# Two typed slabs in place of one byte slab: shared buffers and later loads in a sandwich transformer layer on 8 cores

## The chip, the cores and the metric

The kernel runs on the 8 cores of one Trainium2 chip, with one launch for the whole layer. Each core works for itself: there is no transfer between cores. The metric is the device time of the slowest core in microseconds.

## The reference

The layer takes `x` of 4 x 2048 tokens x 2048 features. Attention has 32 query heads and 8 key/value heads of 64, with rotary embedding and a causal mask; the FFN has 8-bit weights held as integers, 8192 wide.

```python
x = x + layernorm(attention(layernorm(x), wq, wk, wv, wo))
x = x + layernorm(ffn(layernorm(x), gate_w, gate_scale, up_w, up_scale, down_w, down_scale))
# attention: q, k, v = x@wq, x@wk, x@wv; rope(q), rope(k); softmax(q k^T / 8, causal) v; @wo
# ffn: W = (w_int - 128) * scale per output row; h = silu(x Wg^T) * (x Wu^T); h Wd^T
```

## The kernel before

A core owns 1024 of the 2048 tokens of one batch entry: 64 of every 128. It computes K and V for all 2048 tokens of that entry and everything else for its own. There is no scheduler: each engine's program is the sequence of its blocks in the order in which the Python code emits them, and all that holds engines apart are waits on five counters. `pt`, `pv`, `ps` count PE, DVE and ACT; `dx` counts the transfers issued by SP, `dw` those issued by POOL. `Prog.inc` adds to a counter and `wait_ge(c.dx.sem, c.dx.n)` waits for every transfer issued on that queue so far. A name such as `v_krope[t]` is the value of `pv` at which a step is done. So a wait emitted on a queue also holds everything that is emitted on that queue behind it.

On chip memory is one byte tensor, `slab`, of 197,120 bytes per partition, in which each buffer is a bitcast view at a fixed offset, and beside it a number of small tensors: the rotary tables `qcos_s`, `qsin_s`, `kcos_s`, `ksin_s`, the scales `gsc_s`, `usc_s`, the selection matrix `selm` and others.

The stages, in order:

- **Prelude** (`emit_prelude`): SP loads ten small constants and tables and waits for all (L267, L268); POOL loads `eye_b`.
- **Phase A** (`emit_phase_a`): POOL loads `wk_p`, then `wv_p`. 16 tiles t of 128 tokens: SP loads `xt` (L326, two buffers; tile t waits for `v_ln1[t-2]`), DVE takes statistics (L222, L226), ACT computes `rstd` (L230, L233), DVE normalizes (L346). Two tiles later, `emit_a1(t)`: PE transposes (L359), ACT copies out (L368, L372), PE projects K and V (L383, L386), DVE applies the rotation from `kcos_s` and `ksin_s` and keeps the key norms (L246 to L407, whose last is `v_krope[t]`), PE transposes K (L420), ACT copies it out. The loop emits `emit_a0(t)` and then `emit_a1(t - 2)`, so `emit_a1(7)` stands behind `emit_a0(9)` and ahead of `emit_a0(10)` on every queue.
- **Phase A2** (`emit_phase_a2`): for each half h, POOL loads 1024 columns of `wq_p` once phase A is done; PE projects Q (L484), DVE rotates it and sums its squares, PE transposes it, ACT copies it out.
- **Phase B** (`emit_phase_b`): a bound of the scores per row, then 32 heads `qh`, 16 blocks `cc` of 128 keys each: PE scores (L756), ACT exp (L768), DVE mask (L777), PE product with V (L719 to L726). At a head's end DVE copies the denominators (L792, L793) and the product (L795, L796) into `rawatt`, ACT inverts the denominators (L802, L805), and inside the next head (`emit_tail`, ahead of block 4) PE spreads the reciprocals over partitions (L683, L685), DVE copies them to `rbs` (L692) and multiplies into `att_fm` (L698). `rbs` and both `rawatt` lie on partitions 64 to 127.
- **Phase C** (`emit_phase_c`): the output projection (L871, POOL loads `wo_p` in two halves), then 8 blocks p of 128 tokens: SP loads `xown` to `xo` (L926), DVE adds the layernorm (L947, L951) into `x2t`, SP stores it to `x2scr` (L960), and it is normalized again, transposed and copied to `ln3_fm`.
- **Phase D** (`emit_phase_d`): column sums of `ln3_fm` on PE (L1034), spread and scaled (L1043, L1050, L1057), which carry the zero point of 128; then 64 blocks `ib`: POOL loads `wg_p` and `wu_p` (L1080, L1082, one after the other), PE computes gate and up (L1098, L1103), DVE subtracts (L1117, L1119), ACT applies silu (L1125), DVE multiplies (L1132). Then sums over `hdn` (L1142), the down scales spread over partitions (L1173, copied by L1180), and the down projection in 64 loads of `wd_p` (L1194, L1208), each quarter closed by a product with `m128f` (L1214).
- **Phase E** (`emit_phase_e`): 8 blocks p: SP loads the kept rows from `x2scr` to `x2r` (L1255), DVE takes statistics of `y`, normalizes into `ot` (L1274) and adds `x2r` (L1278), SP stores `ot` (L1285). Every load and store on SP waits for all dx transfers before it.

## Time and profile before

| | us |
|---|---|
| median of 2 runs | 3516.13 (3512.64 to 3519.62) |
| the profiled execution | 3343.91 |
| its span, slowest core (core 2) | 3342.4 |
| its spans, all cores | 3312.1 to 3342.4 |

| engine, core 2 | busy us | share of the span |
|---|---|---|
| PE | 2406.5 | 72% |
| PE weight loads (beside PE) | 1075.6 | 32% |
| DVE | 960.6 | 29% |
| ACT | 664.1 | 20% |
| POOL | 108.0 | 3% |

PE is busy for most of the span, but the stages differ, so a share of the whole span says little about one place. The views used are: the busy time by stretch, which shows the limit of each stage; the timeline, in which each instruction stands with its start, its duration and, in brackets, how long its engine was idle before and what released it; and the groups by form, which give the mean duration of one instruction. Times count from the start of the span.

### The profile page before, as it was taken

What the parts mean: (1) busy time and instruction counts of PE and PEld (TensorE: products, weight loads), DVE (VectorE), ACT (ScalarE), POOL (GpSimd) and SP (SyncE); (2) the same over time, 40 slices, a digit from 0 to 9 for tenths busy, and PEclk for the clock granted to TensorE, in tenths of its full rate; (3) what the DMA queues carried; (4) which work ended last, traced back from release to release, by engine and by line L of the source; (5) the groups of instructions that cost most, each with busy time, mean ns of one, the idle gap of its engine ahead of it and who ended that gap; (6) DMA issues with size and microseconds to landing.
All of it is one profiled execution on the core that took longest, in us unless ns stands there. A gap on an engine that the chain in (4) does not pass through costs nothing.

```text
span 3342.4 us, 28537 instructions; the slowest of 8 cores (3312.1 to 3342.4 us)
## 1 busy us (share of the span) xinstructions
PE 2406.5 (72%) x10358; PEld 1075.6 (32%) x10358; DVE 960.6 (29%) x1647; ACT 664.1 (20%) x1307; POOL 108.0 (3%) x203
## 2 busy tenths in 40 slices
PE   2555355356777777655717999999999989999960
PEld 1222122122322332222413444444444434444420
DVE  4444133233444444400173222222222200000024
ACT  1222112114666666500121000000000000000000
POOL 0000000000000000000000000000000000000000
PEclk9777687676676676678958999999999999999885
DMA  5110300300000000033044444444444424334324
GB/s 138 50 51 26 49 2 3 48 0 1 1 1 1 1 1 1 13 51 51 0 151 89 76 77 77 76 78 76 76 76 76 70 40 74 63 63 76 58 69 163
DMA packets 44984, 174.90 MB, mean 52 GB/s; under 512 B 5033, under 2 KB 5425, under 8 KB 38449
## 3 DMA queue, kind: packets, MB, share of 16 engines
q0 software_dynamic: 36336, 121.68, 22.0%
q1 hardware_dynamic: 8514, 51.40, 4.3%
q8 instruction: 88, 1.44, 0.2%
q14 instruction: 46, 0.38, 0.0%
HBM read 277.89 MB, written 16.78 MB: 88 GB/s over the span
## 4 chain that ended last, share of the span: by engine, by line
PE 66%; DVE 13%; DMA 9%; ACT 7%; issue 5%; DVEq 0%; ACTq 0%; SPq 0%; POOLq 0%
PE psA L1098 13%; PE psB L1103 13%; PE psA L1208 7%; PE psB L1208 7%; PE psA L484 5%; PE psA L871 3%; ACT slab L768 3%; PE psA L756 3%; PE psB L383 2%; PE psB L722 2%; PE psB L386 2%; DMA slab<-wq_p 2%; DMA slab<-wo_p 2%; PE psB L719 2%; DVE stat L222 2%
## 5 line engine op out<-in xcount | busy, mean ns | idle before, releaser
L1098 PE MATMUL psA<-slab 128*128 128x512 bf16 x2048 | 464.5, 380 | 2.9 <-DVE slab L1057 1.5
L1103 PE MATMUL psB<-slab 128*128 128x512 bf16 x2048 | 462.9, 379 | 0.0
L1208 PE MATMUL psA<-slab 128*128 128x512 bf16 x1024 | 268.2, 385 | 17.9 <-DVE slab L1225 15.4
L1098 PEld LDWEIGHTS psA<-slab 128*128 128x128 bf16 x2048 | 200.3, 98 | 247.4 <-issue 8.5
L1103 PEld LDWEIGHTS psB<-slab 128*128 128x128 bf16 x2048 | 200.4, 98 | 241.7
L1208 PE MATMUL psB<-slab 128*128 128x512 bf16 x1024 | 266.8, 383 | 0.0
L768 ACT ACTIVATE slab<-psA 128x1024 bf16<-128x1024 f32 (+7 forms) x352 | 226.2, 660 | 135.6 <-PE psA L756 132.7
L1117 DVE TENSOR_TENSOR slab<-psA,slab 128x1024 f32<-128x1024 f32 x64 | 78.4, 1224 | 574.0 <-PE psB L1103 574.0
L1125 ACT ACTIVATE slab<-slab,gsc_s 128x1024 bf16<-128x1024 f32 x64 | 73.5, 1148 | 830.7 <-DVE slab L1119 830.7
L484 PE MATMUL psA<-slab 128*128 128x512 bf16 x512 | 171.0, 508 | 64.4 <-DMA slab<-wq_p 64.4
L719 PE MATMUL psB<-slab 128*65 128x512 bf16 (+3 forms) x256 | 114.6, 448 | 123.7 <-DVE slab L777 123.2
L756 PE MATMUL psA<-slab 65*128 65x512 bf16 (+3 forms) x544 | 184.6, 416 | 4.9 <-DMA slab<-rowv 4.8
L383 PE MATMUL psB<-slab 128*128 128x512 bf16 x256 | 115.6, 452 | 84.8 <-ACT slab L372 84.8
L871 PE MATMUL psA<-slab 128*128 128x512 bf16 x512 | 119.7, 388 | 68.2 <-DMA slab<-wo_p 68.2
L230 ACT ACTIVATE lntmp<-mv,epsv 128x1 f32<-128x1 f32 x40 | 12.0, 300 | 749.1 <-DVE mv L226 749.1
L1225 DVE TENSOR_TENSOR slab<-psA,slab 128x512 bf16<-128x512 f32 x16 | 9.9, 682 | 491.3 <-PE psB L1214 491.3
L1208 PEld LDWEIGHTS psA<-slab 128*128 128x128 bf16 x1024 | 101.0, 99 | 147.0 <-issue 29.6
L722 PE MATMUL psB<-slab 128*65 128x512 bf16 x256 | 145.2, 567 | 0.0
L1208 PEld LDWEIGHTS psB<-slab 128*128 128x128 bf16 x1024 | 101.3, 99 | 124.4 <-issue 6.3
L513 PE MATMUL psB<-eye_b,slab 128*128 128x128 bf16 x128 | 13.9, 238 | 148.0 <-DVE qn L500 148.0
L386 PE MATMUL psB<-slab 128*128 128x512 bf16 x256 | 114.7, 448 | 0.0
L484 PEld LDWEIGHTS psA<-slab 128*128 128x128 bf16 x512 | 62.2, 125 | 159.2 <-issue 138.4
(126 smaller groups left out, 2172.2 us busy)
## 6 DMA issues: line engine op xcount, KB each, us to landing
slab<-wg_p POOLq DMA_DIRECT2D x64, 512.0 KB, 5.2
slab<-wu_p POOLq DMA_DIRECT2D x64, 512.0 KB, 5.9
slab<-wd_p POOLq DMA_DIRECT2D x64, 512.0 KB, 5.2
slab<-xb SPq DMA_DIRECT2D x16, 1024.0 KB
slab<-wq_p POOLq DMA_DIRECT2D x2, 4096.0 KB, 33.8
slab<-xown SPq DMA_DIRECT2D x8, 1024.0 KB
slab<-wo_p POOLq DMA_DIRECT2D x2, 4096.0 KB, 33.0
x2scr<-slab SPq DMA_DIRECT2D x8, 1024.0 KB
```

What stands on the lines that cost most here:

```text
L383: e.matmul(c.bank(4), fm[t % 2][:, dm * 128:(dm + 1) * 128], c.wk_b[:, dm * 512:(dm + 1) * 512], start=(dm == 0), stop=(dm == 15))
L386: ins = e.matmul(c.bank(5), fm[t % 2][:, dm * 128:(dm + 1) * 128], c.wv_b[:, dm * 512:(dm + 1) * 512], start=(dm == 0), stop=(dm == 15))
L484: ins = e.matmul(c.bank(ob), c.pairfm[:, dm * 1024 + p * 128:dm * 1024 + (p + 1) * 128], wqh[:, dm * 1024 + ob * 512:dm * 1024 + (ob + 1) ...
L719: e.matmul(pvb[0][:, p0 * 128:512], lhs, pbf[:, OFFC[cc]:OFFC[cc] + wA], start=(cc == 0), stop=(cc == 7), skip_group_check=True)
L722: ins = e.matmul(pvb[1][:, 0:512], lhs, pbf[:, OFFC[cc] + wA:OFFC[cc] + N], start=(cc == 0), stop=(cc == 15), skip_group_check=True)
L756: ins = e.matmul(s2[si][:, half * 512:half * 512 + n], c.k65[:, kv * 2048 + cc * 128:kv * 2048 + (cc + 1) * 128], c.q65[:, qh * 1024 + p0 ...
L768: ins = e.activation(out=pbuf[qh % 2][:, OFFC[cc]:OFFC[cc] + N], in_=s2[si][:, 0:N], func=ACT.Exp, bias=0.0, scale=1.0)
L871: ins = e.matmul(c.bank(idx % 2), woh_buf[:, dm * 1024 + do * 128:dm * 1024 + (do + 1) * 128], c.att_fm[:, dm * 1024 + grp * 512:dm * 1024 ...
L1098: e.matmul(gbank[:, half * 512:(half + 1) * 512], wgt[ib % 2][:, hc * 128:(hc + 1) * 128], c.ln3_fm[:, hc * 1024 + half * 512:hc * 1024 + ...
L1103: ins = e.matmul(ubank[:, half * 512:(half + 1) * 512], wut[ib % 2][:, hc * 128:(hc + 1) * 128], c.ln3_fm[:, hc * 1024 + half * 512:hc * 1 ...
L1117: ins = e.tensor_tensor(out=gtmp[:], in0=gbank, in1=c.cs3[:, :], op=OP.subtract)
L1208: ins = e.matmul(c.bank(tt), c.hdn[:, ic * 1024 + tt * 128:ic * 1024 + (tt + 1) * 128], wdt[gi % 3][:, ici * 512:(ici + 1) * 512], start=( ...
```

## The change

The byte slab becomes two slabs of fixed types: `slb`, 92,288 bf16 columns, and `slf`, 5,632 float32 columns. Buffers that were bitcast views become slices. The float32 slab is small, so more buffers share space, some are dropped, and several small tensors move into it:

- The K tables hold half their columns. SP loads the first half in the prelude, and the second in phase A, emitted behind `emit_a1(7)`; tile 8's rotation waits for it.
- The Q tables and `selm` are no longer loaded in the prelude but by POOL at the start of phase A2, ahead of `wq_p`, with a wait for them. `gsc_s` and `usc_s` are loaded by POOL ahead of `wg_p[0]`, with a wait.
- `rawatt` is gone: DVE copies the product with V straight to `att_fm` and multiplies it there in place. `rbs` becomes two buffers, on partitions 0 to 63 for even heads and 64 to 127 for odd ones. One wait of DVE moves from ahead of L792 to ahead of L692, and one is added ahead of L698.
- `xo` and `x2t` have one buffer each in place of two, with waits to match.
- `m128f` is set right before the copy of the down scales. The copy to `s3` waits for the dx transfers.
- `ot` is gone: in phase E DVE works in halves of 1024 columns, normalizing into `ln4b` and adding into `x2r`, which is stored.

```diff
--- before.py
+++ after.py
-        c.qcos_s = sb("qcos_s", [128, 256], F32)
-        c.qsin_s = sb("qsin_s", [128, 256], F32)
-        c.kcos_s = sb("kcos_s", [128, 512], F32)
-        c.ksin_s = sb("ksin_s", [128, 512], F32)
-        c.gsc_s = sb("gsc_s", [128, 64], F32)
-        c.usc_s = sb("usc_s", [128, 64], F32)
...
-        SLAB = 197120
-        c.slab = top.enter_context(nc.sbuf_tensor("slab", [128, SLAB], mybir.dt.uint8))
-
-        def view(off, cols, dt, parts=128):
-            esz = mybir.dt.size(dt)
-            return c.slab[0:parts, off:off + cols * esz].bitcast(dt)
-
...
-        c.rbs = c.slab[64:128, 188928:193024].bitcast(F32)
-        c.rawatt = [c.slab[64:128, 184832:186880].bitcast(BF16),
-                    c.slab[64:128, 186880:188928].bitcast(BF16)]
...
-        c.xo = [view(147968, 2048, F32), view(156160, 2048, F32)]
-        c.x2t = [view(164352, 2048, F32), view(172544, 2048, F32)]
...
-        c.x2r = [view(32768, 2048, F32), view(40960, 2048, F32)]
-        c.ot = [view(49152, 2048, F32), view(57344, 2048, F32)]
...
+        c.slb = top.enter_context(nc.sbuf_tensor("slb", [128, NBELS], BF16))
+        c.slf = top.enter_context(nc.sbuf_tensor("slf", [128, NFELS], F32))
+
+        def viewb(off, cols, parts=128):
+            return c.slb[0:parts, off:off + cols]
+
+        def viewf(off, cols, parts=128):
+            return c.slf[0:parts, off:off + cols]
+
...
+        c.xt = [viewf(0, 2048), viewf(2048, 2048)]
+        c.rt1 = viewf(4096, 512)
+        c.rt2 = viewf(4608, 512)
+        c.kcos_s = viewf(5120, 256)
+        c.ksin_s = viewf(5376, 256)
+        c.qcos_s = viewf(0, 256)
+        c.qsin_s = viewf(256, 256)
+        c.qt1 = viewf(4096, 512)
...
+        c.qn2 = viewf(2048, 256)
+        c.selm = viewf(2304, 256, parts=8)
+        c.sqt = viewf(4096, 128)
+        c.sq2 = viewf(4224, 128)
+        c.dens = viewf(0, 1024, parts=1)
+        c.lntmp2 = viewf(1024, 1024, parts=1)
+        c.rbs2 = [c.slf[0:64, 2560:3584], c.slf[64:128, 2560:3584]]
...
+        c.xo = [viewf(0, 2048)] * 2
+        c.x2t = [viewf(2048, 2048)] * 2
+        c.gsc_s = viewf(5120, 64)
+        c.usc_s = viewf(5184, 64)
...
+        c.us = c.ubf
+        c.y = viewb(0, 16384)
+        c.gtmp = viewf(0, 1024)
+        c.cs3 = viewf(2048, 1024)
+        c.s3 = viewf(3072, 1024, parts=1)
+        c.sdn = viewf(3072, 1024, parts=1)
+        c.m128f = viewf(2048, 512, parts=1)
+        c.dsc_s = viewf(0, 2048, parts=1)
+        c.dsc_bc = viewf(0, 2048)
+        c.x2r = [viewf(0, 2048), viewf(2048, 2048)]
+        c.ln4b = viewf(4096, 1024)
...
     @block.sync
     def _(e):
         for dst, srcap in [(c.eye_f, c.eye), (c.mA, c.maskA), (c.mB, c.maskB),
-                           (c.qcos_s, c.qcos), (c.qsin_s, c.qsin),
-                           (c.kcos_s, c.kcos), (c.ksin_s, c.ksin),
-                           (c.gsc_s, c.gsc), (c.usc_s, c.usc),
-                           (c.selm, c.selmap)]:
+                           (c.kcos_s, c.kcos[:, 0:256]),
+                           (c.ksin_s, c.ksin[:, 0:256])]:
             c.dx.inc(e.dma_start(out=dst[:], in_=srcap), 16)
         e.wait_ge(c.dx.sem, c.dx.n)
...
-        e.memset(c.onescb[:], 1.0)
-        c.pv.inc(e.memset(c.m128f[:], -128.0))
+        c.pv.inc(e.memset(c.onescb[:], 1.0))
...
-            c.pv.inc(_rope(c, e, c.bank(4), 8, c.kcos_s[:, t * 32:(t + 1) * 32],
-                           c.ksin_s[:, t * 32:(t + 1) * 32], krot[:], rt1, rt2))
+            if t == 8:
+                e.wait_ge(c.dx.sem, c.dx_kh)
+            tm = t % 8
+            c.pv.inc(_rope(c, e, c.bank(4), 8, c.kcos_s[:, tm * 32:(tm + 1) * 32],
+                           c.ksin_s[:, tm * 32:(tm + 1) * 32], krot[:], rt1, rt2))
...
+        if t == 7:
+            @block.sync
+            def _(e):
+                e.wait_ge(c.pv.sem, v_krope[7])
+                e.wait_ge(c.dx.sem, c.dx.n)
+                c.dx.inc(e.dma_start(out=c.kcos_s[:], in_=c.kcos[:, 256:512]), 16)
+                c.dx.inc(e.dma_start(out=c.ksin_s[:], in_=c.ksin[:, 256:512]), 16)
+                c.dx_kh = c.dx.n
...
             if h == 1:
                 e.wait_ge(c.pt.sem, t_q[(0, 7, 1)])
             e.wait_ge(c.dw.sem, c.dw.n)
+            if h == 0:
+                c.dw.inc(e.dma_start(out=c.qcos_s[:], in_=c.qcos), 16)
+                c.dw.inc(e.dma_start(out=c.qsin_s[:], in_=c.qsin), 16)
+                c.dw.inc(e.dma_start(out=c.selm[:], in_=c.selmap), 16)
+                e.wait_ge(c.dw.sem, c.dw.n)
             ins = e.dma_start(out=wqh[:].rearrange("p (a b) -> p a b", a=16),
                               in_=c.wq_p[:, :, h * 1024:(h + 1) * 1024])
             dwq[h] = c.dw.inc(ins, 16)
...
             e.wait_ge(c.pt.sem, t_bc[qh])
-            ins = e.tensor_copy(out=c.rbs[:, :], in_=s2[0][0:64, 0:1024])
+            if (qh - 2) in v_att:
+                e.wait_ge(c.pv.sem, v_att[qh - 2])
+            rbsv = c.rbs2[qh % 2]
+            ins = e.tensor_copy(out=rbsv, in_=s2[0][0:64, 0:1024])
             v_rbs[qh] = c.pv.inc(ins)
             e.wait_ge(c.pv.sem, v_rbs[qh])
+            e.wait_ge(c.pv.sem, v_raw[qh])
             j = qh // 2
             r0 = (qh % 2) * 64
             dst = c.att_fm[r0:r0 + 64, j * 1024:(j + 1) * 1024]
-            ins = e.tensor_tensor(out=dst[:, :], in0=c.rawatt[qh % 2][:, :],
-                                  in1=c.rbs[:, :], op=OP.mult)
+            ins = e.tensor_tensor(out=dst[:, :], in0=dst[:, :],
+                                  in1=rbsv, op=OP.mult)
             v_att[qh] = c.pv.inc(ins)
...
-            if (qh - 2) in v_att:
-                e.wait_ge(c.pv.sem, v_att[qh - 2])
             e.tensor_copy(out=c.dens[0:1, 0:512], in_=pvb[0][64:65, 0:512])
             ins = e.tensor_copy(out=c.dens[0:1, 512:1024], in_=pvb[1][64:65, 0:512])
             v_dens[qh] = c.pv.inc(ins)
-            e.tensor_copy(out=c.rawatt[qh % 2][:, 0:512], in_=pvb[0][0:64, 0:512])
-            ins = e.tensor_copy(out=c.rawatt[qh % 2][:, 512:1024], in_=pvb[1][0:64, 0:512])
+            j = qh // 2
+            r0 = (qh % 2) * 64
+            dst = c.att_fm[r0:r0 + 64, j * 1024:(j + 1) * 1024]
+            e.tensor_copy(out=dst[:, 0:512], in_=pvb[0][0:64, 0:512])
+            ins = e.tensor_copy(out=dst[:, 512:1024], in_=pvb[1][0:64, 0:512])
...
-            if p < 2:
+            if p == 0:
                 e.wait_ge(c.pv.sem, c.v_att_all)
                 e.wait_ge(c.pt.sem, bar_pt)
                 e.wait_ge(c.ps.sem, bar_ps)
             else:
-                e.wait_ge(c.pv.sem, v_x2[p - 2])
+                e.wait_ge(c.pv.sem, v_x2[p - 1])
...
+            if p >= 1:
+                e.wait_ge(c.pv.sem, v_l3[p - 1])
...
+        e.wait_ge(c.dx.sem, c.dx.n)
         c.pv.inc(e.tensor_copy(out=s3[:], in_=c.psA[0:1, 0:1024]))
...
+            if ib == 0:
+                c.dw.inc(e.dma_start(out=c.gsc_s[:], in_=c.gsc), 16)
+                c.dw.inc(e.dma_start(out=c.usc_s[:], in_=c.usc), 16)
+                e.wait_ge(c.dw.sem, c.dw.n)
             c.dw.inc(e.dma_start(out=wgt[ib % 2][:], in_=c.wg_p[ib]), 16)
             e.wait_ge(c.dw.sem, c.dw.n)
             ins = e.dma_start(out=wut[ib % 2][:], in_=c.wu_p[ib])
...
         e.wait_ge(c.pt.sem, c.pt.n)
+        e.wait_ge(c.pv.sem, v_h[63])
+        e.memset(c.m128f[:], -128.0)
         c.pv.inc(e.tensor_copy(out=c.dsc_bc[:], in_=c.psA[:, :]))
...
-            c.pv.inc(e.tensor_scalar(out=ot[p % 2][:], in0=yv[:, p, :],
-                                     scalar1=c.mv[:, 0:1], scalar2=c.rstd[:, 0:1],
-                                     op0=OP.subtract, op1=OP.mult))
-            e.wait_ge(c.pv.sem, c.pv.n)
-            ins = e.tensor_add(ot[p % 2][:], ot[p % 2][:], x2r[p % 2][:])
-            v_o[p] = c.pv.inc(ins)
+            for half in range(2):
+                c.pv.inc(e.tensor_scalar(
+                    out=c.ln4b[:], in0=yv[:, p, half * 1024:(half + 1) * 1024],
+                    scalar1=c.mv[:, 0:1], scalar2=c.rstd[:, 0:1],
+                    op0=OP.subtract, op1=OP.mult))
+                e.wait_ge(c.pv.sem, c.pv.n)
+                sl = x2r[p % 2][:, half * 1024:(half + 1) * 1024]
+                v_o[p] = c.pv.inc(e.tensor_add(sl, sl, c.ln4b[:]))
+                if half == 0:
+                    e.wait_ge(c.pv.sem, v_o[p])
...
-            c.dx.inc(e.dma_start(out=c.out[p * 128:(p + 1) * 128, :], in_=ot[p % 2][:]), 16)
+            c.dx.inc(e.dma_start(out=c.out[p * 128:(p + 1) * 128, :], in_=x2r[p % 2][:]), 16)
```

## Rows read from the trace of the kernel before

**Rows 1.** Spans by core: span in us, mean granted TensorE clock.

```profile
core 2: 3342.4 us, clock 0.830
```

**Rows 2.** Windows: stretch, length, PE, PEld, DVE, ACT, POOL busy, PEclk, DMA share, GB/s.

```profile
780.00:1415.00 635.00, 459.64 (x1610) 191.93 (x1610) 276.44 (x709) 382.79 (x587) 0.00 (x0) 0.68 0.00 1
...
1779.00:2716.00 937.00, 926.98 (x4260) 415.31 (x4259) 235.52 (x195) 75.83 (x66) 67.67 (x128) 0.99 0.43 72
...
3235.00:3342.40 107.40, 0.00 (x0) 0.00 (x0) 50.36 (x56) 3.98 (x16) 0.00 (x0) 0.50 0.43 156
```

**Rows 3.** Timeline, start: start us, us, engine, line, instruction [idle before].

```profile
1.56 0.66 POOL L272 DMA_DIRECT2D eye_b<-eye  x1 [0.86 <-POOLq L44]
...
5.50 0.53 POOL L301 DMA_DIRECT2D slab<-wk_p  x1 [3.28 <-DMA eye_b<-eye]
...
43.69 1.87 PE L359 MATMUL psA<-eye_b,slab 128*128 128x128 bf16 x16 [43.69 <-DMA slab<-wv_p]
```

**Rows 4.** Chain that ended last, start of phase A: start us, us, what.

```profile
43.87 5.63 DMA slab<-xb
```

**Rows 5.** Timeline, phase A around tile 10; xN rows start at their first.

```profile
181.92 63.30 SPq L326 DMA_DIRECT2D slab<-xb  x4
...
218.42 0.17 DVE L407 TENSOR_TENSOR knm<-knm,kn 128x8 f32<-128x8 f32 x1
...
219.10 2.46 DVE L222 BATCH_NORM_STATS2 stat<-slab 128x6 f32<-128x512 f32 x4
...
222.41 0.20 ACT L233 ACTIVATE rstd<-lntmp 128x1 f32<-128x1 f32 x1
...
222.63 2.05 ACT L368 CAST slab<-psA 128x512 bf16<-128x512 f32 x4
```

**Rows 6.** Timeline, start of phase A2.

```profile
421.00 4.90 PE L484 MATMUL psA<-slab 128*128 128x512 bf16 x16 [34.89 <-DMA slab<-wq_p]
...
426.01 0.42 DVE L246 TENSOR_TENSOR slab<-psA,qcos_s 128x256 f32<-128x256 f32 x1 [39.94 <-PE psA L484]
```

**Rows 7.** Timeline, start of phase D.

```profile
1780.01 0.55 POOL L1080 DMA_DIRECT2D slab<-wg_p  x1 [237.30 <-issue]
...
1787.67 1.21 DVE L1043 COPY slab<-psA 1x1024 f32<-1x1024 f32 x1 [13.15 <-PE psA L1034]
...
1791.09 1.22 DVE L1057 TENSOR_SCALAR slab<-psB 128x1024 f32<-128x1024 f32 x1 [2.21 <-PE psB L1050]
...
1791.20 0.53 POOL L1080 DMA_DIRECT2D slab<-wg_p  x1 [5.09 <-DMA slab<-wu_p]
...
1792.46 5.24 PE L1098 MATMUL psA<-slab 128*128 128x512 bf16 x16 [1.48 <-DVE slab L1057]
```

**Rows 8.** Timeline, start of the down projection.

```profile
2724.34 1.86 PE L1208 MATMUL psA<-slab 128*128 128x512 bf16 x4 [2.54 <-DVE slab L1180]
```

**Rows 9.** Groups by form: line, engine, shapes | busy us, mean ns | idle.

```profile
L1117 DVE TENSOR_TENSOR slab<-psA,slab 128x1024 f32<-128x1024 f32 x64 | 78.4, 1224 | 574.0 <-PE psB L1103 574.0
...
L280 DVE MEMSET m128f<- 1x512 f32 x1 | 0.5, 485 | 0.1
```

**Rows 10.** Timeline, one block of phase E.

```profile
3254.59 1.34 DVE L1274 TENSOR_SCALAR slab<-slab,mv,rstd 128x2048 f32<-128x2048 bf16 x1 [6.91 <-DMA slab<-x2scr]
...
3256.03 2.29 DVE L1278 TENSOR_TENSOR slab<-slab 128x2048 f32<-128x2048 f32 x1
...
3258.46 0.34 SPq L1285 DMA_DIRECT2D out<-slab  x1
```

**Rows 11.** Timeline, DVE in the attention: one instruction per head, four of them.

```profile
990.26 1.22 DVE L692 COPY slab<-psA 64x1024 f32<-64x1024 f32 x1 [0.95 <-PE psA L685]
...
1008.89 1.22 DVE L692 COPY slab<-psA 64x1024 f32<-64x1024 f32 x1 [0.95 <-PE psA L685]
...
1260.33 1.22 DVE L692 COPY slab<-psA 64x1024 f32<-64x1024 f32 x1 [0.95 <-PE psA L685]
...
1280.51 1.22 DVE L692 COPY slab<-psA 64x1024 f32<-64x1024 f32 x1 [0.95 <-PE psA L685]
```

76 lines of the change are left out of this document (29 added, 47 removed).

## The prediction

> **What bounds the kernel now.** I read the spans by core first, then the busy time by stretch, then the timeline at each place that the diff touches. Core 2 is the slowest, with a span of 3342.4 us and a mean granted clock of 0.830 [rows 1]; the profiled execution took 3343.9 us. The median of the runs shown is 3516.13 us, 172 us (5.2%) more. No row says where these 172 us lie, so the sum is made against 3343.9 and then laid on the median.
>
> The stages run one after the other. The attention (785 to 1415 us) is a loop of latencies between PE, ACT and DVE in which no engine is full: PE 460, ACT 383, DVE 276 of 635 us, at a granted clock of 0.68 of the full 2.4 GHz, so a mix of both levels [rows 2]. The FFN's up part is PE's: 927 of 937 us busy, at 0.99 [rows 2]. In the last 107.4 us PE does nothing, DVE works 50.4 us, and the transfer engines are busy for 0.43 of it [rows 2]: store and load take turns with DVE. So the question for each edit is whether it sits in PE's full stretches (where only PE counts) or in one of the serial places, where each microsecond shows.
>
> **Prelude.** SP issues 5 small loads instead of 10, so the first x tile comes a little sooner. But PE's first matmul waits for wv_p, at 43.69 us, behind eye_b and wk_p on POOL's queue [rows 3], which the edit leaves alone. Value 0. The bounds are 0 and a gain of 2.5 us: some 0.6 MB less to move beside wk_p, where an x tile of 1 MB takes 5.63 us alone [rows 4], and not all of it falls beside wk_p.
>
> **Phase A, the second half of the K tables.** The cost lies in where SP's block was put. Between load x[9] and load x[10] SP gets a wait on v_krope[7] and two loads. Load x[10] hung on v_ln1[8] until now and went out at 181.92 us; v_krope[7] ends at 218.42 + 0.17 = 218.59 [rows 5]. Then come two issues, about 0.5 us each, and load x[10] at about 219.65. A tile alone takes 5.63 us [rows 4]: landing at 225.3, and up to 1.4 us later if the 256 KB of tables share the engines with it (a quarter of 5.63). DVE started its stats of tile 10 at 219.10 [rows 5]. That is 6.2 to 7.6 us late; I take 6.7. Who is behind it: rstd of tile 10 on ACT, and on ACT the copies L368 of tile 8, which start right behind rstd's second step (222.41 + 0.20) at 222.63 [rows 5]; PE's projections of tile 8 wait for those copies. rstd is what they wait for already, so no cover is left, and the stall passes in full, once: **+6.7**. Load x[11] then goes out near 226, long before its own stats one tile later; nothing else is late.
>
> **Phase A2, tables and selm on POOL.** Three small loads and a wait for them now stand ahead of the first wq_p load, for which PE waits 34.89 us [rows 6]: nothing covers them. The nearest row is eye_b on the same queue: 0.66 us of issue, 3.28 us of idle until it has landed, and wk_p's issue starts 3.94 us after eye_b's [rows 3]. Two more issues at 0.6 us make 5.1 us at the least; the upper bound takes the wait behind a 512 KB weight load, 5.09 us [rows 7], and one more microsecond for the tables' 256 KB: 8.0. These loads carry more than eye_b and far less than a weight tile, so I stay near the lower end: **+5.5**. The Trainium skill, DMA: Bandwidth & Descriptors, section "Anatomy of one DMA — SWDGE (gpsimd) path", gives about 2.0 us plus bytes by 436 GB/s for one such load; by it this term would be an estimated 4.2 us and the whole sum 1 to 3 us less. eye_b's row contradicts it by 1.3 us, and the row is used.
>
> **Phase D, gate and up scales on POOL.** Two loads and a wait stand ahead of wg_p[0], which went out at 1780.01 [rows 7]. By eye_b's row it goes 3.94 + 0.55 = 4.5 us later. The cover: wu_p[0] had landed by 1791.20, while DVE's L1057, for which PE waits too, ended at 1791.09 + 1.22 = 1792.31 [rows 7]. 1.1 us are hidden: **+3.4** (bounds 2.8, if the second issue costs nothing, and 5.2, with 5.09 for the wait). Block 1's pair (two loads of 5.09 + 0.53) then lands near 1807, before PE asks for it one block (927 / 64 = 14.5 us) after 1795.9: no second stall. A rule speaks against moving loads to POOL: by the Trainium skill, SBUF — State Buffer, the warning about the "DVE blocks DMA" trap, the descriptors of gpsimd loads aren't written while DVE runs in a two-port mode. DVE sat idle for 39.94 us before 426.01 and for 13.15 us before 1787.67 [rows 6, 7], so by this trace it would add nothing.
>
> **m128f.** The memset moves from the start to a place right before the copy L1180, for which PE waits [rows 8]; it took 485 ns [rows 9]: **+0.5**.
>
> **Phase E, halves.** Each of the 8 blocks was L1274 1.34, a gap of 0.10, L1278 2.29, and the store's issue 0.13 later: 3.87 us from 3254.59 to 3258.46 [rows 10]. A tensor_tensor over 1024 takes 1.22 (L1117 [rows 9]), one over 2048 takes 2.29, so 1.05 ns an element and 0.15 fixed. L1274 at 1.34 for 2048 goes at half that per element: 1.07, and 0.27 fixed; 1024 take 0.81 (bounds 0.67, half of it, and 1.22, as slow as L1117). Two halves: 2 x (0.81 + 0.10 + 1.22) + 0.10 + 0.13 = 4.49, so 0.62 more per block. SP's order is load, store, load, and each waits for the one before, with DVE between: all 8 count, **+4.9** (bounds 2.7 and 11.5).
>
> **Attention.** One wait on DVE is taken from before L792 and two are put beside L692 and L698, each on work long done; DVE's gaps with a met wait are the 0.10 us of [rows 10], so at most 0.1 x 32 = 3 us either way. Value 0. But the heads aren't alike: from L692 to L692 one takes 18.63 us and another 20.18 [rows 11], the ends of the 30 gaps between whole heads, with the same work. If the shift of everything before them moved all heads to one end, it would be half the spread, 0.8 x 32 = 25 us, either way.
>
> **Edits at nothing.** Typed slabs for byte views: each instruction keeps element types and shapes, so the rows' durations stand, and buffers that now share space are held apart by written waits, so only these count. Phase C's single `xo` and `x2t`: SP's order is load p, store p, load p+1, and load p+1 waits for store p, so it never ran ahead; the new waits are met when reached. The wait on all dx before the s3 copy: the last store of x2scr is cover enough behind the transposes and L1034; without that cover it is at most a tile's 5.6 us. Phase E in place: store p has ended before load p+1 goes out, so the missing `ot` blocks nothing.
>
> **Sum:** 6.7 + 5.5 + 3.4 + 0.5 + 4.9 = 21.0 us. On the profiled execution 3343.9 + 21 = 3365; on the median 3516.1 + 21 = **3537 us**, 0.6% more. The terms are latencies of transfers and DVE, so I lay them on the median unscaled.
>
> **The rivals.** (1) *The stalls are hidden.* If tile 10 were needed later than I read and POOL's loads landed in a microsecond, phase E's 4.9 and some of the rest stay: about +9, 3525 us. Against it: consumers already wait at these places [rows 5, 6]. Chance 0.12. (2) *The attention's rhythm moves.* For it: heads of equal work differ by 1.5 us; against it: 32 heads even it out. At its ends 3512 and 3562 us; chance 0.12, evenly split. (3) *Slower beyond 2%: the in-place product.* L795 and L796 now write `att_fm`, L698 reads and writes the same addresses, and even heads have their reciprocals on partitions 0 to 63. If L692 and L698 took double, 2.44 us more per head with the masks L777 queued behind them and PE waiting for the masks, 32 heads cost 78 us: 3615 us. It decides from 1.5 us per head on, (70 - 21) / 32. Against it: shapes and types are unchanged. Chance 0.05. (4) *The median moves to the profiled level.* The profiled execution ran 172 us below the median; if the changed kernel's runs stood there, 3365 us would be shown, 4.3% faster, nothing of it due to the diff. Chance 0.04.
>
> **How the numbers follow.** The sum's own case has the remaining 0.67. Within 2% of 3516 (3446 to 3586; two percent is about what a measurement of this kernel can tell from no change) lie the sum, rival 1 and rival 2: 0.91. Faster has 0.04, slower 0.05. The sum's own bounds: A 6.2 to 7.6, A2 5.1 to 8.0, D 2.8 to 5.2, E 2.7 to 11.5, prelude -2.5 to 0, so 3531 to 3549. The range takes in the attention's rhythm on both sides with a little for the waits: 3508 to 3572; it leaves out rivals 3 and 4.
>
> **What would show it.** In the profile after: the stats of tile 10 begin near 225.8, their wait put down to the x load, and phase A ends 6 to 7 us later; PE's wait for wq_p grows from 35 to about 40 us; PE's first L1098 waits some 3.4 us for a weight transfer instead of for L1057; a memset of 0.49 us before L1180's copy; phase E's halves at 0.81 and 1.22, its blocks 0.6 us further apart. The attention from its first L692 to its last stays within 10 us, with L692 and L698 at 1.22. I am wrong if L777, L692 or L698 get longer, if PE's full stretches change by more than their first wait, or if the timed runs stand at another level than before.

## The result and the profile after

| | before | after |
|---|---|---|
| median of all runs | 3381.6 us (20 runs, from 3339.9) | 3362.2 us (21 runs, from 3348.1) |
| ratio of after to before, with its 95% interval | | 1.0035 [1.0022, 1.0049] |
| profiled execution | 3343.9 us | 3367.5 us |
| its spans, all cores | 3312.1 to 3342.4 us | 3315.7 to 3365.9 us |

The changed kernel is slower by 0.35%, which is some 12 us of 3345, and counts as the same by 2%. The direction and the class are as predicted; the number, 3537 us, and its range are not: 3362 us lies far below 3508. In a good part of the runs of either kernel one die shows a lower granted clock and the time is longer, which by their times holds for both runs behind the 3516 us; the others take 3340 to 3350 us for the kernel before, and the ratio is made of such runs alone.

The spans of the two slowest cores and the medians of the two dies of the changed kernel; they answer to [rows 1]:

```profile
core 5: 3361.6 us, clock 0.826
core 6: 3365.9 us, clock 0.826
...
die 0 (median of its cores): 3332.4 us, clock 0.833
die 1 (median of its cores): 3354.5 us, clock 0.827
```

Its slowest cores are not typical ones. On core 6 the down projection took 541.6 us and on core 7 538.4, from the load of the down scales to the first load of phase E, against 521.8 on the median core. The windows of core 5 and then of core 6, the same stretch of that stage (cores 0 and 4 are at 0.95 there like core 5, core 7 at 0.88 like core 6):

```profile
core 5: us, PE busy (x) PEld busy (x) DVE busy (x) ACT busy (x) POOL busy (x), PEclk, DMA share, GB/s
...
3050.00:3200.00 150.00, 144.87 (x636) 64.43 (x635) 4.87 (x8) 0.00 (x0) 10.04 (x19) 0.95 0.42 69
```

```profile
core 6: us, PE busy (x) PEld busy (x) DVE busy (x) ACT busy (x) POOL busy (x), PEclk, DMA share, GB/s
...
3050.00:3200.00 150.00, 144.06 (x574) 61.84 (x585) 4.87 (x8) 0.00 (x0) 8.98 (x17) 0.88 0.38 63
```

PE is as busy in both and gets fewer matmuls done at the lower clock (574 and 636). The repetition of the changed kernel (`e9`) does not have this. It is a part of why the profiled executions stand 23.5 us apart where the timed runs stand 12. From here on stages are compared as means over the eight cores, each stage from its first instruction to that of the next (worked out from the timelines of all cores):

| stage, mean over the cores, us | before | after |
|---|---|---|
| start to PE's first matmul | 44.6 | 45.2 |
| to the first load of `wq_p` (phase A; after, the POOL loads too) | 341.6 | 353.4 |
| phase A2 and the bounds of phase B | 393.2 | 391.0 |
| attention and the first half of phase C | 880.9 | 875.4 |
| first store of `x2scr` to first load of `wg_p` | 107.1 | 110.5 |
| gate and up | 935.2 | 933.5 |
| down projection | 521.0 | 526.1 |
| phase E | 101.0 | 104.0 |

The windows that answer to [rows 2], core 6:

```profile
core 6: us, PE busy (x) PEld busy (x) DVE busy (x) ACT busy (x) POOL busy (x), PEclk, DMA share, GB/s
780.00:1415.00 635.00, 461.63 (x1621) 192.45 (x1619) 274.58 (x713) 382.86 (x590) 0.00 (x0) 0.70 0.00 1
1779.00:2716.00 937.00, 919.37 (x4171) 415.17 (x4253) 235.36 (x194) 78.06 (x70) 68.77 (x130) 0.99 0.42 72
3259.00:3365.90 106.90, 0.00 (x0) 0.00 (x0) 54.15 (x73) 3.98 (x16) 0.00 (x0) 0.50 0.40 157
```

Attention and FFN look much as before (the same stretch of time begins some 9 us earlier in the program here). DVE's 54.15 us in the last window stand against 50.36 [rows 2]: the halves.

**Tile 10** (timeline, answers to [rows 5]):

```profile
216.91 0.17 DVE L408 TENSOR_TENSOR knm<-knm,kn 128x8 f32<-128x8 f32 x1
...
217.21 0.33 SPq L444 DMA_DIRECT2D slf<-kcos  x1
...
217.59 0.43 SPq L445 DMA_DIRECT2D slf<-ksin  x1
...
218.16 12.85 SPq L324 DMA_DIRECT2D slf<-xb  x3
...
225.59 2.47 DVE L223 BATCH_NORM_STATS2 stat<-slf 128x6 f32<-128x512 f32 x4 [7.91 <-DMA slf<-xb]
...
228.91 0.20 ACT L234 ACTIVATE rstd<-lntmp 128x1 f32<-128x1 f32 x1
229.13 2.05 ACT L366 CAST slb<-psA 128x512 bf16<-128x512 f32 x4
```

The load of tile 10 goes out behind the two table loads, DVE sits idle for 7.91 us before the statistics (5.6 to 8.5 on the eight cores, 6.9 on average; nothing was there before), and ACT's copies of tile 8 stand right behind that rstd.

**The POOL loads** (timeline, POOL and PE at the start of phase A2, then POOL, DVE and PE at the start of phase D; they answer to [rows 6, 7]):

```profile
395.38 0.54 POOL L479 DMA_DIRECT2D slf<-qcos  x1 [370.75 <-PE psB L421]
...
396.45 0.52 POOL L481 DMA_DIRECT2D slf<-selmap  x1
398.85 1.17 POOL L483 DMA_DIRECT2D slb<-wq_p  x1 [1.87 <-DMA slf<-selmap]
431.47 5.72 PE L499 MATMUL psA<-slb 128*128 128x512 bf16 x15 [36.78 <-DMA slb<-wq_p]
```

```profile
1782.41 0.57 POOL L1104 DMA_DIRECT2D slf<-gsc  x1 [234.77 <-issue]
...
1782.97 0.55 POOL L1105 DMA_DIRECT2D slf<-usc  x1
...
1785.72 0.54 POOL L1107 DMA_DIRECT2D slb<-wg_p  x1 [2.19 <-DMA slf<-usc]
...
1793.31 1.22 DVE L1080 TENSOR_SCALAR slf<-psB 128x1024 f32<-128x1024 f32 x1 [2.21 <-PE psB L1073]
...
1797.36 3.19 PE L1125 MATMUL psA<-slb 128*128 128x512 bf16 x7 [4.16 <-DMA slb<-wu_p]
```

`wq_p` goes out 3.5 us behind the first POOL issue on this core (3.9 on the mean of the eight) and `wg_p` 3.3 us. PE's first gate matmul, which waited for the sums before (1.48 <-DVE in [rows 7]), now waits for a weight transfer.

**`m128f` and phase E** (timeline, answers to [rows 8, 10]):

```profile
2725.10 0.48 DVE L1208 MEMSET slf<- 1x512 f32 x1 [5.74 <-PE psA L1200]
2725.51 2.22 DVE L1209 COPY slf<-psA 128x2048 f32<-128x2048 f32 x1
```

```profile
3273.11 0.32 SPq L1284 DMA_DIRECT2D slf<-x2scr  x1
3277.91 0.81 DVE L1304 TENSOR_SCALAR slf<-slb,mv,rstd 128x1024 f32<-128x1024 bf16 x1 [6.05 <-DMA slf<-x2scr]
3278.83 1.23 DVE L1310 TENSOR_TENSOR slf<-slf 128x1024 f32<-128x1024 f32 x1
...
3282.22 2.46 DVE L223 BATCH_NORM_STATS2 stat<-slb 128x6 f32<-128x512 bf16 x4
3282.43 0.34 SPq L1318 DMA_DIRECT2D out<-slf  x1
```

From the start of the first half to the issue of the store are 4.52 us, against 3.87 before.

### The profile page after: what moved, and what is told of

It reads as the page before. It is cut to its first block, busy times and chain, and to the rows that moved or that the text cites. A ratio compares the mean times of both kernels' runs of the same rounds, so it can differ in the third digit from the quotient of the medians.

```text
span 3365.9 us, 28447 instructions; the slowest of 8 cores (3315.7 to 3365.9 us)
## 1 busy us (share of the span) xinstructions
PE 2413.8 (72%) x10190; PEld 1082.1 (32%) x10358; DVE 962.8 (29%) x1663; ACT 664.7 (20%) x1307; POOL 110.7 (3%) x208
## 4 chain that ended last, share of the span: by engine, by line
PE 66%; DVE 13%; DMA 8%; ACT 7%; issue 5%; DVEq 0%; ACTq 0%; SPq 0%; POOL 0%; POOLq 0%
PE psA L1125 13%; PE psB L1130 13%; PE psA L1237 7%; PE psB L1237 7%; PE psA L499 5%; PE psA L891 3%; ACT slb L787 3%; PE psA L775 3%; PE psB L384 2%; PE psB L741 2%; PE psB L381 2%; DMA slb<-wq_p 2%; DMA slb<-wo_p 2%; PE psB L738 2%; DVE stat L223 2%
## 5 line engine op out<-in xcount | busy, mean ns | idle before, releaser
L1125 PE MATMUL psA<-slb 128*128 128x512 bf16 x2007 | 461.6, 380 | 6.3 <-DMA slb<-wu_p 4.2
L1130 PE MATMUL psB<-slb 128*128 128x512 bf16 x2007 | 459.9, 379 | 2.2
L1237 PE MATMUL psA<-slb 128*128 128x512 bf16 x1002 | 274.6, 396 | 20.4 <-DVE slb L1254 15.8
L1125 PEld LDWEIGHTS psA<-slb 128*128 128x128 bf16 x2048 | 200.8, 98 | 247.6 <-issue 7.7
L1130 PEld LDWEIGHTS psB<-slb 128*128 128x128 bf16 x2048 | 200.4, 98 | 241.6
L1237 PE MATMUL psB<-slb 128*128 128x512 bf16 x1004 | 273.6, 394 | 1.2
L787 ACT ACTIVATE slb<-psA 128x1024 bf16<-128x1024 f32 (+7 forms) x352 | 226.7, 660 | 135.3 <-PE psA L775 132.7
L1144 DVE TENSOR_TENSOR slf<-psA,slf 128x1024 f32<-128x1024 f32 x64 | 78.4, 1225 | 574.6 <-PE psB L1130 574.6
L1152 ACT ACTIVATE slb<-slf 128x1024 bf16<-128x1024 f32 x64 | 73.4, 1148 | 831.1 <-DVE slb L1146 831.1
L499 PE MATMUL psA<-slb 128*128 128x512 bf16 x499 | 169.3, 509 | 66.4 <-DMA slb<-wq_p 64.7
L738 PE MATMUL psB<-slb 128*65 128x512 bf16 (+3 forms) x256 | 115.0, 449 | 123.5 <-DVE slb L796 123.5
L775 PE MATMUL psA<-slb 65*128 65x512 bf16 (+3 forms) x544 | 184.4, 416 | 4.8 <-DMA slb<-rowv 4.8
L384 PE MATMUL psB<-slb 128*128 128x512 bf16 x256 | 115.9, 453 | 87.7 <-ACT slb L370 87.7
L891 PE MATMUL psA<-slb 128*128 128x512 bf16 x496 | 119.2, 390 | 63.3 <-DMA slb<-wo_p 62.5
L1237 PEld LDWEIGHTS psA<-slb 128*128 128x128 bf16 x1024 | 103.2, 101 | 155.2 <-issue 61.1
L741 PE MATMUL psB<-slb 128*65 128x512 bf16 x256 | 146.0, 570 | 0.0
L1237 PEld LDWEIGHTS psB<-slb 128*128 128x128 bf16 x1024 | 103.4, 101 | 131.2 <-issue 36.1
L528 PE MATMUL psB<-eye_b,slb 128*128 128x128 bf16 x128 | 13.7, 236 | 148.0 <-DVE slf L515 148.0
L381 PE MATMUL psB<-slb 128*128 128x512 bf16 x241 | 108.0, 448 | 10.6 <-ACT slb L370 10.6
L499 PEld LDWEIGHTS psA<-slb 128*128 128x128 bf16 x512 | 62.2, 125 | 159.6 <-issue 138.9
```

The lines of the kernel that those rows point to most:

```text
L381: e.matmul(c.bank(4), fm[t % 2][:, dm * 128:(dm + 1) * 128], c.wk_b[:, dm * 512:(dm + 1) * 512], start=(dm == 0), stop=(dm == 15))
L384: ins = e.matmul(c.bank(5), fm[t % 2][:, dm * 128:(dm + 1) * 128], c.wv_b[:, dm * 512:(dm + 1) * 512], start=(dm == 0), stop=(dm == 15))
L499: ins = e.matmul(c.bank(ob), c.pairfm[:, dm * 1024 + p * 128:dm * 1024 + (p + 1) * 128], wqh[:, dm * 1024 + ob * 512:dm * 1024 + (ob + 1) ...
L738: e.matmul(pvb[0][:, p0 * 128:512], lhs, pbf[:, OFFC[cc]:OFFC[cc] + wA], start=(cc == 0), stop=(cc == 7), skip_group_check=True)
L741: ins = e.matmul(pvb[1][:, 0:512], lhs, pbf[:, OFFC[cc] + wA:OFFC[cc] + N], start=(cc == 0), stop=(cc == 15), skip_group_check=True)
L775: ins = e.matmul(s2[si][:, half * 512:half * 512 + n], c.k65[:, kv * 2048 + cc * 128:kv * 2048 + (cc + 1) * 128], c.q65[:, qh * 1024 + p0 ...
```

## The experiments

The theory is the prediction's sum: the change adds five small serial stalls, each worth its own microseconds, and nothing else. Its rivals: the stalls are covered (rival 1), the attention moves (rival 2), the in-place product costs (rival 3). All ratios are to the kernel before, with 95% intervals.

### The second half of the K tables, taken out of the way and put in alone

`e1` is the changed kernel with the table loads emitted one tile later, behind the load of tile 10; the load of tile 11 waits for them.

```diff
-        if t == 7:                       # in emit_a1
-            <SP: wait v_krope[7]; load kcos, ksin second half>
+        if t == 10:                      # in the loop, behind emit_a0(10)
+            emit_kh()
```

> The changed kernel with one block moved: SP's wait for v_krope[7] and its two loads of the second half of the K tables are emitted behind the load of x tile 10 instead of ahead of it, and the load of tile 11 waits for the tables. Theory (the queue position costs, not the tables): DVE no longer idles before its stats of tile 10 (5.6 to 8.5 us on the eight cores of the changed kernel, mean 6.9), phase A from PE's first matmul to the first wq_p issue shrinks by 6.9 us in the mean over cores, and the kernel's time goes from a ratio of 1.0035 to about 1.0015. Rival (the tables' transfer or the missing half costs): the stall only moves to tile 8's rotation or to tile 11, and phase A stays within 2 us of the changed kernel's.

Measured: 1.0019 [1.0006, 1.0033]. SP (timeline of `e1`, core 4) and then DVE:

```profile
215.70 0.33 SPq L444 DMA_DIRECT2D slf<-kcos  x1
216.08 0.42 SPq L445 DMA_DIRECT2D slf<-ksin  x1
218.86 5.48 SPq L324 DMA_DIRECT2D slf<-xb  x2
```

```profile
216.08 2.47 DVE L223 BATCH_NORM_STATS2 stat<-slf 128x6 f32<-128x512 f32 x4
```

The tables still go out at the same place, but tile 10 is there, and its statistics begin without idle time (no bracket). From tile 1's key norm to the last one the eight cores take 294.2 us on the mean, against 293.8 before, and 300.4 to 303.7 with the block where the change has it (`e2`, `e9` and the changed kernel). In the stretch that the expectation names, PE's first matmul to the first `wq_p`, it is 343.3 us, 10.1 less than in the changed kernel and 5.3 less than in its repetition `e9`.

`e11` is the reverse: the kernel before, with the tables loaded in halves at the change's place.

```diff
-                           (c.kcos_s, c.kcos), (c.ksin_s, c.ksin),
+                           (c.kcos_s[:, 0:256], c.kcos[:, 0:256]),
+                           (c.ksin_s[:, 0:256], c.ksin[:, 0:256]),
...
+        if t == 9:
+            <SP: wait v_krope[7]; load the second halves>
```

> The kernel before with the K tables loaded in halves exactly where the change does it (SP's wait for v_krope[7] and two loads behind the load of tile 9), into the full-size tables. Theory (the stall of tile 10 passes in full to phase A's end): DVE stalls 5.5 to 8.5 us before tile 10, phase A from PE's first matmul to the first wq_p issue grows from 341.6 us by 6 to 7, ratio 1.0020. Rival (part of it is made up in the following tiles, as PE runs at another mix of its two clock levels): phase A grows by 4 us or less.

Measured: 1.0018 [1.0007, 1.0029], and 302.0 us from tile 1's key norm to the last, 8.2 more than before. In the stretch that the expectation names it is 347.4 us, 5.9 more than before: the part of it that lies ahead of tile 1's norm is 2.5 us shorter in `e11`, whose prelude loads half of the K tables less. Its DVE on the slowest core, the place of tile 10:

```profile
224.88 2.47 DVE L222 BATCH_NORM_STATS2 stat<-slab 128x6 f32<-128x512 f32 x4 [7.60 <-DMA slab<-xb]
```

So this part alone makes the stall and is worth 6 to 8 us, whichever kernel it stands in. On a single core it comes in two sizes. Without the stall a core takes 293.2 to 293.9 us from norm to norm, and now and then 296.1; with it 299.7 to 300.5, or 302.8 to 303.6, so some 6.5 or 9.5 us more (two cores of the changed kernel took longer still, see below). How many cores do which differs from run to run, and why was not tested.

### The loads moved to POOL

`e2` is the changed kernel with the Q tables, `selm` and the two scales loaded by SP at the end of phase A, on buffers that are free by then.

```diff
-                c.dw.inc(e.dma_start(out=c.qcos_s[:], in_=c.qcos), 16)   # and qsin, selm
-                e.wait_ge(c.dw.sem, c.dw.n)
...
+        e.wait_ge(c.pv.sem, v_ln1[15])                                   # on SP, behind phase A
+        c.dx.inc(e.dma_start(out=c.qcos_s[:], in_=c.qcos), 16)          # and qsin, selm
+        e.wait_ge(c.pv.sem, v_krope[15])
+        c.dx.inc(e.dma_start(out=c.gsc_s[:], in_=c.gsc), 16)             # and usc
```

> The changed kernel with the Q tables, selm and the two scale tables loaded by SP at the end of phase A (behind ln1[15] and krope[15]) instead of by POOL ahead of wq_p and wg_p[0]. Theory: the three POOL loads cost about 4 to 5 us in front of wq_p and the two about 2.2 us on PE in front of the first gate matmul (3.3 us of POOL time less 1.1 us of cover), so about 6 to 7 us come back, and the ratio to the kernel before falls from 1.0035 to about 1.0015. Rival (the transfers are hidden by something else): phase A2's start and phase D's start don't move against phase A's end, and the time stays.

Measured: 1.0037 [1.0021, 1.0053], from 7 runs, where 1.0015 was expected. The time didn't show it; the stages did. From the last key norm to PE's first Q matmul the cores take 32.6 us (before 33.2, after 36.7), and from POOL's first issue to the first gate matmul 13.0 us (before 13.4, after 14.7). Over all kernels without the POOL loads these are 32.6 to 34.4 and 12.9 to 13.7 us, over the three with them (after, `e1`, `e9`) 36.7 to 37.6 and 14.7 to 14.8. The start of phase D in `e2`:

```profile
1777.41 0.55 POOL L1112 DMA_DIRECT2D slb<-wg_p  x1 [234.46 <-issue]
...
1788.30 1.22 DVE L1089 TENSOR_SCALAR slf<-psB 128x1024 f32<-128x1024 f32 x1 [2.21 <-PE psB L1082]
1789.31 0.53 POOL L1112 DMA_DIRECT2D slb<-wg_p  x1 [5.54 <-DMA slb<-wu_p]
1790.05 4.70 PE L1130 MATMUL psA<-slb 128*128 128x512 bf16 x15 [1.86 <-DVE slf L1089]
```

PE waits for DVE's sums again, as in [rows 7]. The two terms are real, 3.5 to 4 us and 1.3 us, but together they are smaller than the width of this interval (0.32%, 10.7 us): the ratio of `e2` alone decides nothing.

`e10` has both mends, `e1`'s and `e2`'s:

> The changed kernel with both mends of the tables (K tables behind the load of tile 10, Q tables, selm and scales by SP at the end of phase A) and phase E as in the change. Theory (what is left is phase E's halves and the memset, 4 to 5.5 us): ratio 1.0010 to 1.0018, phase A as before within 3 us. Rival (the mend of the Q tables and scales gives nothing, as its own timing of 1.0037 seemed to say): the same as with the K tables' mend alone, 1.0019 or more.

Measured: 1.0042 [1.0007, 1.0077]. The interval holds the expected 1.0010 to 1.0018, the rival's 1.0019 and more, and nearly everything else. Its stages agree with the two mends (294.2 us in phase A, 33.8 us at the Q projection, 13.6 us at the FFN's start). As a timing it is inconclusive.

### The halves of phase E

`e3` is the kernel before with phase E done in halves, the sum written into `x2r`.

```diff
-            c.pv.inc(e.tensor_scalar(out=ot[p % 2][:], in0=yv[:, p, :], ...))
-            ins = e.tensor_add(ot[p % 2][:], ot[p % 2][:], x2r[p % 2][:])
+            for half in range(2):
+                c.pv.inc(e.tensor_scalar(out=ot[0][:, 0:1024], in0=yv[:, p, <half>], ...))
+                e.wait_ge(c.pv.sem, c.pv.n)
+                v_o[p] = c.pv.inc(e.tensor_add(sl, sl, ot[0][:, 0:1024]))
```

> The kernel before with phase E's output alone done in two halves in place, as in the change. Theory (each block's 0.62 us of DVE is exposed): from the first x2scr load to the last store the mean over cores grows by 4.3 us for seven blocks and 0.6 for the first, 4.9 in all, ratio about 1.0015. Rival (the transfers behind take some of it back: a load that is issued later meets less traffic): 2 to 3.5 us, with the load of a block taking less than its 5.6 us.

Measured: 1.0012 [1.0001, 1.0024]. Phase E takes 105.0 us. Over all kernels with halves (6) it is 103.5 to 105.7, mean 104.7; over those without, with the old order of SP (4), 98.1 to 101.0, mean 99.9: +4.8 us. Its DVE, core 1, the first half of one block:

```profile
3256.66 0.81 DVE L1275 TENSOR_SCALAR slab<-slab,mv,rstd 128x1024 f32<-128x1024 bf16 x1 [6.26 <-DMA slab<-x2scr]
3257.57 1.22 DVE L1281 TENSOR_TENSOR slab<-slab 128x1024 f32<-128x1024 f32 x1
```

`e6` tests why each tenth of a microsecond counts here: the kernel before with its whole rows, but SP issues load p+2 directly behind store p, two loads lie ahead, and the stores count on a counter of their own.

```diff
-            e.wait_ge(c.dx.sem, c.dx.n)
-            c.dx.inc(e.dma_start(out=c.out[...], in_=ot[p % 2][:]), 16)
+            e.wait_ge(c.ds.sem, c.ds.n)
+            ds_o[p] = c.ds.inc(e.dma_start(out=c.out[...], in_=ot[p % 2][:]), 16)
+            if p + 2 < 8:
+                e.wait_ge(c.dx.sem, c.dx.n)
+                c.dx.inc(e.dma_start(out=x2r[p % 2][:], in_=c.x2scr[<block p+2>]), 16)
```

> The kernel before with phase E's loads emitted ahead of the stores on SP: x2r of block p+1 is loaded while DVE works on block p, and the stores count on a counter of their own. Theory (load, DVE and store stand in one chain of 13.1 us a block, so each microsecond of DVE shows): the block falls to 7 to 9 us, DVE's work of 6.7 us or the two transfers, and some 35 us go: ratio 0.989. Rival (the transfer engines are the limit of phase E): the block stays above 11 us.

Measured: 0.9894 [0.9868, 0.9921]. Phase E falls from 101.0 to 61.6 us. The timeline of `e6`:

```profile
3246.52 0.34 SPq L1288 DMA_DIRECT2D out<-slab  x1
...
3250.01 0.32 SPq L1291 DMA_DIRECT2D slab<-x2scr  x1
3250.05 1.34 DVE L1277 TENSOR_SCALAR slab<-slab,mv,rstd 128x2048 f32<-128x2048 bf16 x1 [0.91 <-DMA slab<-x2scr]
...
3253.92 0.34 SPq L1288 DMA_DIRECT2D out<-slab  x1
```

Store to store is 7.4 us here (7.5 on the mean of all blocks and cores, 13.1 before), and 13.4 in the kernel before (3245.06 to 3258.46 on its core 2, the second in [rows 10]); DVE's idle time before L1277 is 0.91 us in place of 6.91 [rows 10]. The stage was a chain of load, DVE and store with nothing beside it, which is why halves at DVE passed in full. The expected saving of some 35 us arrived: the stage is 39.4 us shorter, the timed ratio says 35 us, with 26 to 44 as its interval, and the means of the spans 35.3. The stage and the spans differ by what the profiled execution of `e6` took more ahead of phase E, in code that is the same in both kernels: phase E begins at 3227.5 us in place of 3223.6.

### The attention: the moved wait and the in-place product

`e4` is the kernel before with the wait on `v_att[qh-2]` moved from ahead of the copy of the denominators to ahead of L692.

```diff
-            if (qh - 2) in v_att:
-                e.wait_ge(c.pv.sem, v_att[qh - 2])
             e.tensor_copy(out=c.dens[0:1, 0:512], ...)
...
             e.wait_ge(c.pt.sem, t_bc[qh])
+            if (qh - 2) in v_att:
+                e.wait_ge(c.pv.sem, v_att[qh - 2])
             ins = e.tensor_copy(out=c.rbs[:, :], in_=s2[0][0:64, 0:1024])
```

> The kernel before with one wait of DVE moved, the one on v_att[qh-2], from ahead of the denominators' copy to ahead of the reciprocals' copy; nothing else. In the changed kernel the attention took 1.9 us less on each of the eight cores (627.8 against 629.7 us from the first row store to the first xown load). Theory (a wait that is already met costs its place in the sequencer, some 0.06 us on the head's path, 32 times): 1.9 us less here too. Rival (the product in place, or the reciprocals on the lower partitions, does it): no change here, 629.7 within 0.3 us.

Measured: 0.9996 [0.9982, 1.0011]. From the first store of `rowv` to the first load of phase C the cores take 627.86 us, against 629.71 before. The changed kernel showed 627.81. That looks like the answer, but the same changed code run again (`e9`, below) took 629.52, and `e1`, whose attention is that code too, 629.46. The gaps from head to head (core 0, from the starts of the copy to `rbs`) show why neither is proof:

```
before  18.91 19.75 19.94 18.75 19.54 19.91 19.47 19.10 19.78 18.64 19.42 19.88 18.85 19.36 ...
after   19.25 19.56 19.87 18.65 19.49 19.85 19.10 19.29 19.85 18.57 19.51 20.20 18.35 19.45 ...
e1      19.25 19.53 19.87 18.65 19.49 19.84 19.10 19.29 19.85 18.57 19.51 20.22 19.67 18.90 ...
e9      19.27 19.56 19.88 18.65 19.50 19.86 19.10 19.28 19.86 18.58 19.51 20.21 19.68 18.89 ...
e4      18.90 19.73 18.60 19.31 19.85 18.57 20.25 19.57 19.84 18.71 19.59 19.84 18.95 19.43 ...
```

Short gaps recur at 18.57 us with the moved wait and at 18.63 without, long ones at 19.85 and 19.91, some 0.06 us less a head. But these do not add up to a shorter attention: the changed kernel and its repetition `e9` go together for twelve gaps and then apart, at 18.35 against 19.68, on the same code, `e1` goes with `e9`, and both need 629.6 to 629.8 us for the attention on this core, like the kernel before. Such a step is worth as much as the whole effect.

The cores of all kept traces show how it stands. A core took either 627.7 to 627.9 us or 629.6 to 630.7. The short time came on 18 of the 56 cores with the moved wait (all eight of the changed kernel and of `e4`, one of `e1`, one of `e9`, none of `e2`, `e7` and `e10`) and on none of the 48 without it. The means are 629.3 and 629.9 us. So the short time was seen only with the moved wait, and most cores with the moved wait do not have it; that the wait brings 2 us is not shown. What goes with the step can be read in the windows: in the 13th gap PE's granted clock is 0.78 where it takes 18.35 us (the changed kernel, core 0; `e9`, core 2: 18.34) and 0.67 where it takes 19.68 (`e9`, core 0). Which of the two is the cause of the other was not tested.

`e5` is the kernel before with the product copied to `att_fm` and multiplied there, and `rbs` on the head's own partitions (the inverted denominators move to a part of `kcos_s`, which is dead by then). There is one profiled execution and no ratio.

```diff
-            e.tensor_copy(out=c.rawatt[qh % 2][:, 0:512], in_=pvb[0][0:64, 0:512])
+            dst = c.att_fm[r0:r0 + 64, j * 1024:(j + 1) * 1024]
+            e.tensor_copy(out=dst[:, 0:512], in_=pvb[0][0:64, 0:512])
```

> The kernel before with the attention's product in place in att_fm and the reciprocals on the half that the head writes, as in the change, but with DVE's waits where they were (the inverted denominators use a part of kcos_s, which is dead there). Theory (neither place nor partition costs anything): L692 and the multiply stay at 1.22 us, the gaps between heads run through the same values as before within 0.02 us where they run in the same order, and the attention from the first row store to the first xown load takes 629.7 us. Rival (in place is what gave the changed kernel its 1.9 us): 627.8 us on all cores.

Measured: the attention takes 629.95 us (before 629.71; three cores are at 630.2 to 630.4, the others at 629.7 to 629.8), copy and multiply 1218 and 1220 ns. The changed kernel has the same (groups by form, answer to the L692 and L698 of before):

```profile
L717 DVE TENSOR_TENSOR slb<-slb,slf 64x1024 bf16<-64x1024 bf16 x32 | 39.0, 1220 | 5.5 <-DVE slf L710 5.5
L710 DVE COPY slf<-psA 64x1024 f32<-64x1024 f32 x32 | 38.9, 1217 | 34.1 <-PE psA L700 34.1
```

Rival 3 falls: 1.22 us, where it needed 1.5 us a head more.

### The changed kernel again, and versions that gain

`e9` is the changed kernel without an edit, to see what repeats.

> The changed kernel once more, with one blank line added and nothing else: how far its ratio and its stages repeat. Theory: the ratio lies at 1.003 to 1.0045, DVE's stall before tile 10 is 5.5 to 8.5 us on each core, and the attention takes 627.8 us again, since one program gives one sequence of gaps between heads. Rival (the attention's 1.9 us was luck of that execution): 629 to 631 us on some or all cores.

Measured: 1.0052 [1.0034, 1.007], above the expected 1.003 to 1.0045. Together with 1.0035 [1.0022, 1.0049] this bounds the loss at 7 to 23 us, with 11 to 16 common to both. The stall before tile 10 is there on all cores (5.5 to 6.7 us), POOL's loads take the same 4.0 us, and the attention does not repeat its 627.8 us but on one core (629.7 on the other seven), as the rival said.

`e7` is the changed kernel with both mends and phase E's loads ahead; `e8` is the kernel before with loads ahead in phase E and, in the same manner, in phase C; its attention is that of the kernel before.

> The changed kernel with the two mends of the earlier runs (second half of the K tables behind the load of tile 10; Q tables, selm and scales loaded by SP at the end of phase A) and phase E's loads ahead of the stores, where a load waits for the store of the block that had the buffer. Theory (the terms add): against the changed kernel phase A loses its stall of 6 to 7 us, the two POOL waits of 3.5 to 5 and 2.2 us go, and phase E falls by 30 us or more: ratio 0.991 or less. Rival (each gain is given back at the next wait, as the table loads' seemed to be in the timing of the run that moved them): 0.995 or more.

> The kernel before with loads ahead of stores on SP in phase C too (xo of block p+1 loaded while block p is worked on, stores on their own counter) and in phase E. Theory: phase C's block is at 13.7 us with 12.9 us of DVE and ACT in a row, so 0.8 us a block or 6 us come on top of phase E's 35: ratio 0.987. Rival (phase C's blocks wait for the transposes, not for SP): the same as with phase E alone, 0.989.

Measured: `e7` 0.9898 [0.9877, 0.992], `e8` 0.9891 [0.9869, 0.9913]; with 3306.8 us `e8` is the fastest of all and beats both kernels, but `e6`, `e7` and `e8` can't be told apart. Phase E takes 61.6 us in `e6`, 66.0 in `e7`, which has the halves, and 61.7 in `e8`. In phase C the loads ahead brought nothing, as the rival said: from the first store of `x2scr` to the first `wg_p` 106.8 us against 107.1. There DVE, ACT and PE have the normalization and the transposes between load and store, and in the kernel before (core 2) L947, the first instruction that needs the load, waited for rstd in seven blocks of eight and for the load in one.

## Why the prediction was right, and where it was wrong

| term | predicted us | measured us | from |
|---|---|---|---|
| prelude | 0 (-2.5 to 0) | -1.5 | key norm of tile 1, means of 6 kernels each |
| K tables | 6.7 (6.2 to 7.6) | 6.6 to 8.2 | `e9`, `e2`, `e11`; gone in `e1`, `e10` |
| A2 loads | 5.5 (5.1 to 8.0) | 3.5 to 4 | last key norm to first Q matmul |
| D scales | 3.4 (2.8 to 5.2) | 1.3 | first POOL issue to first gate matmul, mean of the cores |
| `m128f` | 0.5 | 0.5 | its row |
| phase E | 4.9 (2.7 to 11.5) | 4.8 | six kernels against four |
| sum | 21.0 | about 15.7 | |

The sum takes 6.7 us for the K tables and 3.9 for the A2 loads. 15.7 us of 3345 is 1.0047, inside both intervals of the changed kernel; the predicted 21.0 would be 1.0063, above the first of them, 1.0049. The same terms give 1.0027 for `e1` (9.0 us), 1.0031 for `e2` (10.5), 1.0014 for `e3` (4.8) and 1.0020 for `e11` (6.7), and each lies in its measured interval.

**The step that failed is the last one: "laid on the median".** The prediction saw that the median stood 172 us above the profiled execution, said that no row places these 172 us, and then laid the sum on the median. The sum on the profiled execution was in the text, 3365 us, and 3362 us was measured. That these two are so close is in part luck: by the ratio the loss is some 12 us, by the stages some 16, and the sum was 21. Rival 4, at 0.04, was the case that came. The evidence was at hand: all eight spans of the profiled execution lay between 3312.1 and 3342.4 us at 0.83 of full clock [rows 1], every stage of the sum was read there, and against it stood a median of two runs 7 us apart, of which no span by core was known. Two agreeing runs say that they were of one kind, not that others will be. The level should have been split between both, and the range been taken from one to the other, or the chances been stated on the ratio.

**K tables: right, and in full.** The place of the block was read as the cause, and `e1` and `e11` show it. The place (statistics of tile 10), the releaser (the x load), the size and the reason (copies of tile 8 behind rstd of tile 10 on ACT's queue) are in the rows above. That the profiled executions differ by 9.9 us in this stretch, not 6.7, comes from half of the cores: cores 4 and 5, on which six tiles of 21.8 to 22.8 us came before it, took 15.5 and 16.9 us more, cores 0 and 6 some 10, and the other four 6.5 to 6.9; the repetition has 6.6 on the mean.

**Prelude: the missed term.** PE's first matmul came no sooner, as predicted, and from that a value of 0 was drawn; the measured 1.5 us lie within its bounds. But PE's first matmul is not what phase A's pace hangs on there. The rows of the changed kernel, core 0:

```profile
46.87 1.87 PE L357 MATMUL psA<-eye_b,slb 128*128 128x128 bf16 x16 [46.87 <-DMA slb<-wv_p]
...
48.65 2.47 DVE L223 BATCH_NORM_STATS2 stat<-slf 128x6 f32<-128x512 f32 x4 [3.73 <-DMA slf<-xb]
...
51.97 0.20 ACT L234 ACTIVATE rstd<-lntmp 128x1 f32<-128x1 f32 x1
52.08 2.03 ACT L366 CAST slb<-psA 128x512 bf16<-128x512 f32 x4
```

and of the kernel before, core 0:

```profile
45.17 1.86 PE L359 MATMUL psA<-eye_b,slab 128*128 128x128 bf16 x16 [45.17 <-DMA slab<-wv_p]
...
51.21 2.47 DVE L222 BATCH_NORM_STATS2 stat<-slab 128x6 f32<-128x512 f32 x4 [0.85 <-DMA slab<-xb]
...
54.53 0.20 ACT L233 ACTIVATE rstd<-lntmp 128x1 f32<-128x1 f32 x1
54.64 2.03 ACT L368 CAST slab<-psA 128x512 bf16<-128x512 f32 x4
```

PE starts 1.7 us later and the first copies 2.6 us sooner. They stand behind rstd of tile 2, so behind its statistics, which wait for the third x load, and that one does gain from the smaller prelude. On the mean of the cores the first copies start at 50.6 to 51.7 us in the six kernels with the small prelude, at 52.2 in `e11`, which has part of it, and at 52.2 to 53.7 in the other six. It is the very order on ACT's queue that the prediction used for tile 10, and it was not applied to tile 2.

**POOL's loads: mechanism right, size too large.** Both terms took eye_b's 3.28 us [rows 3] for the wait until a small load has landed. The rows above show 1.87 and 2.19 us; over all cores of the three kernels with these loads it is 1.87 to 3.43 us ahead of `wq_p`, 2.3 on the mean, and 1.85 to 2.90 ahead of `wg_p`, 2.1 on the mean. With these, `wq_p` is 3.9 us late on the mean instead of 5.1 or more. The Trainium skill, DMA: Bandwidth & Descriptors, section "Anatomy of one DMA — SWDGE (gpsimd) path", gives about 2.0 us plus the bytes by 436 GB/s, and by it the A2 term was an estimated 4.2 us; the trace agrees with it better than with eye_b's row. That row was of the kernel's first POOL load, with SP's loads beside it; what in that made it slower wasn't tried. In phase D the later `wg_p` also met more cover than the 1.1 us read on core 2: by the same reading the eight cores of the kernel before had -0.1 to 2.5 us, 1.4 on the mean, and on the mean 1.3 us remain of 3.0 to 3.3. The other half microsecond is not explained.

**Phase E: right.** 0.81 and 1.22 us were worked out from fixed and per-element parts of two rows, and both came out to the hundredth; `e6` shows the chain that makes them count.

**The rivals.** Rival 1 (stalls hidden, +9) is refuted by `e1`, `e2` and `e11`, in which the stalls come and go with their cause. Rival 2, a shift of the attention by up to 25 us, did not come: its 1.9 us in one execution were 0.2 in the next. Rival 3 is refuted by L710 and L717. The edits costed at nothing showed no cost that could be told from the spread: gate and up take 933.5 us (935.2 before), the down projection 521.8 on the median core (520.6), and the stretch from the first load of phase C to its first store 247.6 and, in `e9`, 250.5 (251.2; `e3`, `e4`, `e5` and `e6`, with the same code there, 249.5 to 253.5).

## What to carry to other kernels

When a wait is put on a queue, ask what is emitted behind it: here two loads of 128 KB each cost 7 us, not by their own time but because an x tile stood behind them, and putting them one block later made them free. When the timed runs and the profiled execution stand at two levels, predict the ratio first and say for each level what the number would be. And before trimming tenths off a stage, look whether load, work and store simply take turns in it: loads ahead in the last stage were worth 39 us there, eight times what the halves cost.

## What the hardware showed that was not expected

- The attention's head gaps follow one of a few sequences. Cores in the same sequence agree within 0.02 us in most gaps, although each core works for itself and they start 12 to 28 us apart, and a core can leave the sequence of the others in the middle of a run. In `e3` core 5 did so after nine heads and took 0.9 us more over the first 30 gaps; in `e5` three cores did; in `e9` core 2 took 627.9 us and the other seven 629.7. PE's granted clock over the whole stretch is 0.68 to 0.70 [rows 2], a mix of its two levels, 1.2 and 2.4 GHz. Over the first 30 gaps of the changed kernel and of `e9` (core 0) it is 0.77 or 0.78 in those of 18.35 to 19.10 us, except one of 18.89, and 0.67 or 0.68 in all others. That the two go together is read from the windows; which is the cause was not tested.
- A small load on POOL's queue landed in 1.85 to 3.43 us in the middle of the kernel, 2.2 on the mean, and in 3.1 to 3.9 us, 3.4 on the mean, as the kernel's first.
- Cores 6 and 7 of one die ran the down projection 17 to 20 us longer than the median core in one execution, at a clock of 0.88 for a stretch in which the others had 0.95, and not in the next. With the slowest of eight cores as the metric, such an event hides terms of 1 to 5 us; the means of a stage over the cores showed them.
